# A placement of planned steps on five queues, and a third place on chip for the last sequence's results

## The chip, the cores and the metric

One core of a Trainium2 chip runs the whole program. The metric is the device time of one execution in microseconds (us). The engines are PE (TensorE: matmuls and transposes), DVE (VectorE), ACT (ScalarE), POOL (GpSimd) and SP (SyncE, which here only issues DMAs). Each takes its instructions in the order in which they were written for it, and waits at semaphores.

## The reference, cut to what matters

Eight sequences of 512 tokens go through attention and then through a mixture of experts, each between two layernorms and with a residual.

```python
def attention(x, W_q, W_k, W_v, W_o):                 # x: (8, 512, 256), 16 heads of 16
    Q, K, V = (split_heads(x @ W.T) for W in (W_q, W_k, W_v))
    Q, K = rope(Q), rope(K)
    score = where(causal, -inf, einsum('bnqd,bnkd->bnqk', Q, K) / sqrt(16))
    out = einsum('bnqk,bnkd->bnqd', softmax(score), V)
    return merge_heads(out) @ W_o.T

def ffn(x):                                           # 16 experts of width 128, top 4 in 2 of 4 groups
    scores = sigmoid(x @ gate_w.T)
    topk_idx, topk_w = grouped_top4(scores + gate_bias, scores)      # weights normalized, times 2.5
    y = sum over the 4 experts e of a token: w_e * (silu(x @ Wg[e].T) * (x @ Wu[e].T)) @ Wd[e].T
    return x + y + (silu(x @ Ws_g.T) * (x @ Ws_u.T)) @ Ws_d.T

x = x + layernorm(attention(layernorm(x)))
x = x + layernorm(ffn(layernorm(x)))
```

## The kernel before

The program has three stretches. In the first, attention, the shared expert and the routing run for sequence after sequence (0 to 8, called s), as a pipeline over 32 quads of heads (Q = 4s to 4s+3). In the second, expert blocks of 128 rows go through in duos (BT1, BGU, BT2, BDN): 48 duos for group 0 (sequences 0 to 4), then 32 for group 1 (sequences 5 to 7). The results of group 0 are summed and normalized between the duos of group 1; those of group 1 come last, in a third stretch of their own.

**What sets the order.** `make_plan()` gives each step a time in units of its own (12 a sequence, 3 a quad) and sorts them; every engine then walks the one list PLAN and issues its own part of each step. So a number in the tables BEFORE and AFTER moves a step on all engines that have a part in it, SP too. The steps that matter here, by name:

- LX loads x of a sequence (SP). QK 0 and QK 1 are the two halves of queries and keys: products on PE, four rotary products on DVE (L770 to L774), sums on POOL (L669, L671). SPL splits them into a high part (ACT, `part`, which first waits until the store of the half before has landed) and a low part (POOL, L676). SPS stores them to memory (SP, L522). STL is the stacking load of one quad back from there, eight DMAs (SP, L536 to L539).
- S is a score unit on PE with its row maxima on DVE (L781). MT turns a quad's maxima into rows (PE, ACT, DVE L1081) and SP writes them into `q_st` with four small DMAs (L547). ST is the transposed scores unit with its exponential on ACT (L1189); the first ST of a quad waits for that quad's MT rows. AV and OT make the attention output.
- AT and OP are the output projection (AT: low halves of it on DVE, L799). LNA takes the projection's statistics on DVE, POOL the root. LNB is `residual()`: four rows (L819), one sum (L823), and then the statistics of that sum (L803 to L809). LNC makes the normalized rows, HT transposes them.
- DP is `place_rows()` on DVE, SC are its sixteen scatters on POOL (L691). GE is `group_table()` on DVE, with DUM and PAD the zero rows on SP, WE the load of all expert weights (6144 KB).
- PE's first three PSUM places are a ring for S, ST, XT, QK, V, AT, OP, HT, GU and SD: each waits until the step three places before has been read.

**The last stretch.** `sums(g)` lists it: CZ loads z and x1 of a sequence back (SP, L600 and L601), CL the four experts' rows of half a sequence (SP, L613, 1024 KB), CA adds them (for group 1 on PE, L1380, eight products a half, and then DVE L1016), CS takes statistics, CN makes the final rows (DVE L1046, L1049), and SP stores them (L618). `ykt`, `zt` and `x1t` have two places, by s % 2: sequence 7 takes those of sequence 5, so its CL 7 0 and CL 7 1 wait for CN 5 0 and CN 5 1, and CZ 7 waits until both stores of sequence 5 have landed.

## Time and profile before

| | us |
|---|---|
| median of 3 runs | 1031.69 |
| lowest, highest | 1030.8, 1032.27 |
| time of the profiled execution | 1031.85 |
| its span in the profile | 1030.0 |
| PE busy, share of the span | 830.4, 81% |
| DVE busy, share | 654.9, 64% |

The span runs from the first to the last instruction that the profiler saw; 1.85 us of the execution lie around it. Times in the trace are from the span's start. A row of a timeline begins with the start and the duration of an instruction (or of several alike, "x8"), then come the engine, the line, the operation and the tiles (out<-in); the brackets at its end tell how long the engine had been idle, and who released it.

### The profile page before, as it was taken

What the parts mean: (1) busy time and instruction counts of PE and PEld (TensorE: products, weight loads), DVE (VectorE), ACT (ScalarE), POOL (GpSimd) and SP (SyncE); (2) the same over time, 40 slices, a digit from 0 to 9 for tenths busy, and PEclk for the clock granted to TensorE, in tenths of its full rate; (3) what the DMA queues carried; (4) which work ended last, traced back from release to release, by engine and by line L of the source; (5) the groups of instructions that cost most, each with busy time, mean ns of one, the idle gap of its engine ahead of it and who ended that gap; (6) DMA issues with size and microseconds to landing.
All of it is one profiled execution on the core that took longest, in us unless ns stands there. A gap on an engine that the chain in (4) does not pass through costs nothing.

```text
span 1030.0 us, 20612 instructions
## 1 busy us (share of the span) xinstructions
PE 830.4 (81%) x6580; PEld 610.5 (59%) x6580; DVE 654.9 (64%) x1906; ACT 452.2 (44%) x763; POOL 434.8 (42%) x416
## 2 busy tenths in 40 slices
PE   3449887896898798698796887799988999988763
PEld 3326454564565465466464555688877788777521
DVE  4375758687687787777777694554553333877543
ACT  2115544553544455363464555555444455444300
POOL 4431203115425425424522424467567655655610
PEclk9758989899898899898898898899999999998977
DMA  4475744334444443533559422354556667988663
GB/s 164 118 189 149 226 109 126 81 84 138 127 112 116 130 123 118 136 102 98 157 156 304 138 88 91 109 177 150 175 172 217 201 168 265 337 302 305 237 234 123
DMA packets 89175, 168.72 MB, mean 164 GB/s; under 512 B 14704, under 2 KB 56688, under 8 KB 88816
## 3 DMA queue, kind: packets, MB, share of 16 engines
q1 hardware_dynamic: 75248, 128.85, 43.7%
q0 software_dynamic: 13824, 38.55, 9.9%
q8 instruction: 57, 0.93, 0.4%
q14 instruction: 46, 0.38, 0.1%
HBM read 90.15 MB, written 76.68 MB: 162 GB/s over the span
## 4 chain that ended last, share of the span: by engine, by line
PE 27%; DVE 12%; DMA 6%; issue 5%; SPq 4%; POOL 3%; ACT 2%; DVEq 0%; ACTq 0%; POOLq 0%
PE ring L1480 7%; PE ring L1501 3%; DVE nmax L781 3%; DMA xg<-sorted_rows 2%; PE ring L1259 2%; DMA ykt<-expert_rows 2%; PE ring L1466 2%; PE ring L1261 2%; PE ring L1260 2%; POOL expert_rows L699 2%; PE ring L1380 2%; SPq L592 2%; PE ring L1337 1%; DMA expert_rows<-ys,dest 1%; SPq L593 1%
## 5 line engine op out<-in xcount | busy, mean ns | idle before, releaser
L1189 ACT ACTIVATE prob<-ring 128x1024 f32<-128x1024 f32 (+1 forms) x192 | 167.4, 880 | 208.1 <-PE ring L1328 207.8
L781 DVE TENSOR_REDUCE nmax<-ring 128x2 f32<-128x1024 f32 (+3 forms) x256 | 200.8, 818 | 43.5 <-PE ring L1310 41.6
L699 POOL DMA_INDIRECT expert_rows<-ys,dest x160 | 157.7, 985 | 96.9 <-ACT ys L1143 40.5
L691 POOL DMA_INDIRECT sorted_rows<-xr,idx_all x128 | 131.0, 1023 | 79.7 <-DVE xr L940 46.6
L1480 PE MATMUL ring<-we,xh 128*128 x640 | 155.1, 386 | 0.0
L1480 PEld LDWEIGHTS ring<-we,xh 128*128 128x128 f32 x640 | 118.3, 195 | 13.3
L1003 DVE SCALAR_TENSOR_TENSOR sl<-sl,got,ring 128x128 f32<-128x128 f32 x160 | 48.3, 344 | 104.1 <-ACT sl L1241 103.8
L1322 PE MATMUL ring<-maskt_b,halves_b 64*128 64x128 bf16 (+2 forms) x768 | 57.2, 229 | 63.6 <-DVE nmax L781 37.0
L669 POOL TENSOR_TENSOR rot<-rot 128x512 f32<-128x512 f32 x16 | 20.4, 1278 | 204.6 <-DVE rot L773 204.6
L1322 PEld LDWEIGHTS ring<-maskt_b,halves_b 64*128 64x128 bf16 x768 | 22.5, 96 | 133.2 <-DVE nmax L781 53.7
L1337 PE MATMUL ring<-prob,v_sb 128*32 128x512 f32 (+3 forms) x1024 | 97.9, 481 | 1.7 <-ACT prob L1189 1.7
L1303 PE MATMUL ring<-k_st,q_st 48*128 48x512 f32 (+3 forms) x512 | 84.9, 370 | 17.5 <-ACT prob L1189 9.8
L1328 PE MATMUL ring<-q_st,k_st 50*128 50x384 f32 (+3 forms) x512 | 90.0, 389 | 0.0
L1501 PE MATMUL ring<-we,ah 128*128 x320 | 84.4, 387 | 1.3 <-ACT ys L1143 1.3
L1241 ACT ACTIVATE sl<-ring 128x256 f32<-128x256 f32 x80 | 30.7, 383 | 87.7 <-PE ring L1480 87.7
L1303 PEld LDWEIGHTS ring<-k_st,q_st 48*128 48x128 f32 x512 | 49.3, 210 | 29.0 <-ACT prob L1189 18.1
L1143 ACT ACTIVATE ys<-ring 128x512 f32<-128x512 f32 x80 | 47.8, 598 | 40.6 <-PE ring L1501 34.8
L1466 PE MATMUL ring<-kc,xg 128*128 128x128 f32 x320 | 51.0, 284 | 15.9 <-DMA xg<-sorted_rows 15.9
L1310 PE MATMUL ring<-mask_b,halves_b 64*128 64x128 bf16 (+2 forms) x768 | 60.4, 239 | 0.0
L1143 ACT ACTIVATE xh<-ring 128x512 f32<-128x512 f32 x80 | 47.4, 593 | 28.1 <-PE ring L1466 28.0
L1501 PEld LDWEIGHTS ring<-we,ah 128*128 128x128 f32 x320 | 55.2, 193 | 6.8 <-issue 2.1
L1466 PEld LDWEIGHTS ring<-kc,xg 128*128 128x128 f32 x320 | 40.5, 146 | 26.6 <-DMA xg<-sorted_rows 20.0
(194 smaller groups left out, 1673.7 us busy)
## 6 DMA issues: line engine op xcount, KB each, us to landing
xg<-sorted_rows SPq DMA_DIRECT2D x160, 134.0 KB, 2.5
parts<-part SPq DMA_DIRECT2D x32, 512.0 KB, 5.8
ykt<-expert_rows SPq DMA_DIRECT2D x16, 1024.0 KB, 9.4
k_st<-parts SPq DMA_DIRECT2D x64, 128.0 KB, 3.6
q_st<-parts SPq DMA_DIRECT2D x64, 128.0 KB, 3.5
we<-w_exp SPq DMA_DIRECT2D x1, 6144.0 KB, 21.9
sorted_rows<-zeros SPq DMA_DIRECT2D x2, 2144.0 KB, 12.0
sorted_rows<-zeros SPq DMA_DIRECT2D x32, 134.0 KB
```

Of the source, the lines that this page charges most:

```text
L691: pool.indirect_dma_start(out=xs[group_of(s)], out_offset=bass.IndirectOffsetOnAxis(ap=idx_all[:, s, t, k:k + 1], axis=0), in_=xr[:, s % 2 ...
L699: pool.indirect_dma_start(out=yk, out_offset=bass.IndirectOffsetOnAxis(ap=dest[:, j % 8, b:b + 1], axis=0), in_=ys[:, j % NYS, b, :], in_o ...
L781: dve.tensor_reduce(nmax[:, Q % 2, :, pp, qb], slot[:, :, col:col + (qb + 1) * P], AX.X, ALU.max, negate=True).then_inc(s_max, 1)
L1143: act_e.activation(dst, src, ACT.Copy).then_inc(done, 1)
L1189: act_e.activation(prob[:, u % 2, 2 * half:2 * half + 2, 0:width], slot[:, :, 0:width], ACT.Exp, scale=SCALE).then_inc(s_exp, 1)
L1303: pe.matmul(slot[:, par, col:col + width], q_st[r, Q % NQ, pp, q0:q0 + P], k_st[r, Q % NQ, pp, 0:width], start=n == 0, stop=False, skip_gr ...
L1322: pe.matmul(blocks_of(slot[:, par, :], diagonal)[:, :, 0:64 * (h + 1)], halves_b[r, h, :], mask, start=h == 0, stop=False, skip_group_chec ...
L1328: last = pe.matmul(slot[:, par, col:col + width], k_st[r, Q % NQ, half, k0:k0 + P], q_st[r, Q % NQ, half, k0:T], start=False, stop=True, s ...
L1337: last = pe.matmul(O_BANK[32 * j:32 * j + 32, kb * P:T], v_sb[:, s % 2, kb, 4 * q + j, :], prob[:, u % 2, j, col:col + T - kb * P], start= ...
L1466: last = pe.transpose(X_BANK[:, b, k, :], xg[:, j % NXG, b, k * P:(k + 1) * P], ident)
L1480: last = pe.matmul(G_BANK[j % 2][:, b, :], xh[:, j % 2, b, k, :], we_cols[:, bass.ds(columns[j, b] + k * D, D)], start=(k == 0), stop=(k = ...
L1501: last = pe.matmul(Y_BANK[:, b, :], ah[:, j % 2, b, :], we_cols[:, bass.ds(columns.pop((j, b)) + KD * D, D)], start=True, stop=True)
```

## The change

- `residual()` is cut in two: LNB keeps the rows and the sum, the new step LNS takes the statistics. LNB moves from 25.25 to 24.7, LNS stands where LNB stood. POOL's root for it goes with LNS.
- LX, QK, SPL and SPS of both halves move forward by 0.6 to 0.8 units. DP and SC move back by 0.4 (DP is now behind the low halves of AT), GE by 0.45.
- The last sequence has a third place for `ykt`, `zt` and `x1t`, over the weights and operands of the first stretch. For group 1 `sums()` now lists all CZ, then all six CL, and then the sums.

```diff
-BEFORE = [("LX", -25), ("LN", -20.9), ("LNR", -19.2), ("XT", -16), ("QK", 0, -14.6), ("SPL", 0, -13.6), ("SPS", 0, -12.9),
-          ("QK", 1, -12.8), ("SPL", 1, -11.4), ("SPS", 1, -10.6), ("V", -5)]
-AFTER = [("X1L", 18), ("AT", 22), ("OP", 23), ("LNA", 24), ("LNB", 25.25), ("LNC", 26), ("HT", 27),
+BEFORE = [("LX", -25.6), ("LN", -20.9), ("LNR", -19.2), ("XT", -16), ("QK", 0, -15.2), ("SPL", 0, -14.2), ("SPS", 0, -13.5),
+          ("QK", 1, -13.4), ("SPL", 1, -12.1), ("SPS", 1, -11.4), ("V", -5)]
+AFTER = [("X1L", 18), ("AT", 22), ("OP", 23), ("LNA", 24), ("LNB", 24.7), ("LNS", 25.25), ("LNC", 26), ("HT", 27),
...
-AFTER += [("SD", 30.5), ("Z", 30.501), ("CNT", 32.2), ("DP", 33.9)]
-AFTER += [("SC", n // TOPK, n % TOPK, 34.5 + 0.55 * n) for n in range(NT * TOPK)]
+AFTER += [("SD", 30.5), ("Z", 30.501), ("CNT", 32.2), ("DP", 34.3)]
+AFTER += [("SC", n // TOPK, n % TOPK, 34.9 + 0.53 * n) for n in range(NT * TOPK)]
...
+    if end == B:
+
+        steps = [("CZ", g, s) for s in range(first, end)] + [("CL", g, *half) for half in halves]
+        for i, (s, h) in enumerate(halves):
+            steps += [("CA", g, s, h), ("CS", g, s, h)]
+            if i:
+                steps.append(("CN", g, *halves[i - 1]))
+        return steps + [("CN", g, *halves[-1])]
...
-        add(per_seq * (b - 1) + late(b - 1, 34.3) + FILL, "GE", g)
+        add(per_seq * (b - 1) + late(b - 1, 34.75) + FILL, "GE", g)
...
+        cursor[0] = w_low
+        ykt_last = place("ykt_last", [P, NT, TOPK, D])
+        zt_last = place("zt_last", [P, NT, D])
+        x1t_last = place("x1t_last", [P, NT, D])
+        assert cursor[0] <= w_high
...
-        s_cl = [sem(f"parts_back{i}") for i in range(4)]
-        s_cz = [sem(f"residuals_back{i}") for i in range(2)]
+        s_cl = [sem(f"parts_back{i}") for i in range(6)]
+        s_cz = [sem(f"residuals_back{i}") for i in range(3)]
...
+        def home(s):
+
+            return 2 if s == B - 1 else s % 2
+
+        def turn(s):
+
+            return 1 if s == B - 1 else s // 2 + 1
+
+        def back(s):
+
+            if s == B - 1:
+                return ykt_last, zt_last, x1t_last
+            return ykt[:, s % 2, :, :, :], zt[:, s % 2, :, :], x1t[:, s % 2, :, :]
...
             def load_residuals(s):
-                if s >= 2:
-                    sp.wait_ge(s_out[s % 2], 32 * (s // 2))
+                _, z_home, x1_home = back(s)
+                if turn(s) > 1:
+                    sp.wait_ge(s_out[home(s)], 32 * (turn(s) - 1))
...
-                if s >= 2:
+                if turn(s) > 1:
                     sp.wait_ge(s_cn, N_OUT * (2 * (s - 2) + h + 1))
...
-                elif kind in ("LNA", "LNB"):
-                    post_rstd(n, int(kind == "LNB"))
+                elif kind in ("LNA", "LNS"):
+                    post_rstd(n, int(kind == "LNS"))
...
                 dve.tensor_tensor(x1[:, :, :], x1[:, :, :], pr[:, :, :], ALU.add).then_inc(s_ln, 1)
-                dve.wait_ge(s_ln, done + NT + 1)
-                statistics(x1, s_ln, done + NT + 1, st2, mv2, ve2, s_lnv)
+
+            def residual_statistics(s):
+                done = N_LN * s + 3 * NT + 1
+                dve.wait_ge(s_ln, done)
+                statistics(x1, s_ln, done, st2, mv2, ve2, s_lnv)
...
-                pe.wait_ge(s_cl[2 * (s % 2) + h], 16 * (s // 2 + 1))
+                pe.wait_ge(s_cl[2 * home(s) + h], 16 * turn(s))
```

What is not shown replaces `s % 2` by `home(s)` or `back(s)` in the last stretch's functions.

**SP near the start of the program**, from the load of x of sequence 2 to the first rows of maxima (MT 0). `parts<-part` is SPS, `k_st` and `q_st` from `parts` are STL (quads 2 and 3). Before:

```order
L512 DMA x_ln<-x 128x4x256
L522 DMA parts<-part 64x4x512 x2
L536 DMA k_st<-parts 16x1024
L537 DMA k_st<-parts 32x1024
L538 DMA q_st<-parts 32x1024
L539 DMA q_st<-parts 16x1024
...
L522 DMA parts<-part 64x4x512 x2
...
L547 DMA q_st<-mrow 1x8x128 x4
```

and with the change:

```order
L543 DMA x_ln<-x 128x4x256
L553 DMA parts<-part 64x4x512 x4
L567 DMA k_st<-parts 16x1024
L568 DMA k_st<-parts 32x1024
L569 DMA q_st<-parts 32x1024
L570 DMA q_st<-parts 16x1024
...
L578 DMA q_st<-mrow 1x8x128 x4
```

The store of the second half now stands ahead of the eight loads of quad 2, which stood between the two stores; the same happens in each later sequence, where the rows of maxima of quad 4s-5 stood between the two stores as well.

**DVE at the residual of sequence 4** (`x_67` is x1). Before:

```order
L793 TENSOR_TENSOR att<-ring,rden 128x4x64 [waits attention_transposed,denominators]
L781 TENSOR_REDUCE nmax<-ring 128x2 [waits scores] x2
L1081 TENSOR_TENSOR mrow<-ring,mrow 16x128 [waits maxima_high]
L819 TENSOR_SCALAR pr<-pr,mv_91,rstd_93 128x256 [waits ln_rstd]
L819 TENSOR_SCALAR pr<-pr,mv_91,rstd_93 128x256 x3
L823 TENSOR_TENSOR x_67<-x_67,pr 128x1024 [waits ln_steps,x1_loaded]
L803 BN_STATS st_90<-x_67 128x6 [waits ln_steps]
L803 BN_STATS st_90<-x_67 128x6 x3
L807 BN_AGGR mv_91<-st_90 128x2 [waits ln_steps] x4
L809 TENSOR_SCALAR ve_92<-mv_91 128x4 [waits ln_steps]
L781 TENSOR_REDUCE nmax<-ring 128x2 [waits scores]
```

and with the change:

```order
L825 TENSOR_TENSOR att<-ring,rden 128x4x64 [waits attention_transposed,denominators]
L813 TENSOR_REDUCE nmax<-ring 128x2 [waits scores]
L851 TENSOR_SCALAR pr<-pr,mv_91,rstd_93 128x256 [waits ln_rstd]
L851 TENSOR_SCALAR pr<-pr,mv_91,rstd_93 128x256 x3
L855 TENSOR_TENSOR x_67<-x_67,pr 128x1024 [waits ln_steps,x1_loaded]
L813 TENSOR_REDUCE nmax<-ring 128x2 [waits scores]
L1116 TENSOR_TENSOR mrow<-ring,mrow 16x128 [waits maxima_high]
L835 BN_STATS st_90<-x_67 128x6 [waits ln_steps]
L835 BN_STATS st_90<-x_67 128x6 x3
L839 BN_AGGR mv_91<-st_90 128x2 [waits ln_steps] x4
L841 TENSOR_SCALAR ve_92<-mv_91 128x4 [waits ln_steps]
L813 TENSOR_REDUCE nmax<-ring 128x2 [waits scores]
```

Rows and sum are one row-maximum and MT earlier, and these two stand between them and the statistics.

**SP at the end of the program**, from the residuals of sequence 6 on. Before:

```order
L600 DMA zt<-z_rows 128x1024 [waits x1_stored,z_stored,out_stored0]
L601 DMA x1t<-x_rows 128x1024
L613 DMA ykt<-expert_rows 128x2x1024 [waits block_scattered2,final_rows,block_scattered1,block_scattered0]
L613 DMA ykt<-expert_rows 128x2x1024 [waits final_rows] x3
L618 DMA out<-zt 128x2x256 [waits final_rows]
L613 DMA ykt<-expert_rows 128x2x1024 [waits final_rows]
L618 DMA out<-zt 128x2x256 [waits final_rows]
L600 DMA zt<-z_rows 128x1024 [waits x1_stored,z_stored,out_stored1]
L601 DMA x1t<-x_rows 128x1024
L613 DMA ykt<-expert_rows 128x2x1024 [waits final_rows]
L618 DMA out<-zt 128x2x256 [waits final_rows] x4
```

and with the change:

```order
L632 DMA zt<-z_rows 128x1024 [waits x1_stored,z_stored,out_stored0]
L633 DMA x1t<-x_rows 128x1024
L632 DMA zt_last<-z_rows 128x1024 [waits x1_stored,z_stored]
L633 DMA x1t_last<-x_rows 128x1024
L645 DMA ykt<-expert_rows 128x2x1024 [waits block_scattered2,final_rows,block_scattered1,block_scattered0]
L645 DMA ykt<-expert_rows 128x2x1024 [waits final_rows] x3
L645 DMA ykt_last<-expert_rows 128x2x1024 x2
L650 DMA out<-zt 128x2x256 [waits final_rows] x4
L650 DMA out<-zt_last 128x2x256 [waits final_rows] x2
```

All loads of the last sequence stand ahead of the first store, and none of them waits for a result of sequence 5.

## Rows read from the trace of the kernel before

**Rows 1.** Chain that ended last, 955 to 1031 us: start, duration, what.

```profile
970.43 6.08 DMA expert_rows<-ys,dest
...
978.72 2.38 DMA expert_rows<-ys,dest
...
985.96 12.53 PE ring L1380 x24
...
1001.99 2.91 DMA out<-zt
...
1005.77 7.17 DMA ykt<-expert_rows
...
1012.98 5.80 PE ring L1380 x8
```

**Rows 2.** Timeline of the last stretch.

```profile
968.14 0.93 SPq L601 DMA_DIRECT2D x1t<-x_rows  x1
...
998.59 0.69 DVE L1016 TENSOR_TENSOR ykt<-ring,zt 128x512 f32<-128x512 f32 x1
...
1001.94 0.69 DVE L1016 TENSOR_TENSOR ykt<-ring,zt 128x512 f32<-128x512 f32 x1
```

**Rows 3.** Timeline near the start, SP, ACT and PE.

```profile
57.01 1.84 SPq L536 DMA_DIRECT2D k_st<-parts  x1
...
62.26 1.15 ACT L1143 ACTIVATE part<-rot 128x512 fp32r<-128x512 f32 x2 [8.99 <-DMA parts<-part]
...
65.49 1.24 SPq L522 DMA_DIRECT2D parts<-part  x2
...
66.78 1.96 SPq L536 DMA_DIRECT2D k_st<-parts  x1
...
73.20 0.42 SPq L539 DMA_DIRECT2D q_st<-parts  x1
73.67 2.90 SPq L547 DMA_DIRECT2D q_st<-mrow  x4
...
77.83 0.34 PE L1322 MATMUL ring<-maskt_b,halves_b 64*128 64x64 bf16 x4 [5.94 <-DMA q_st<-mrow]
```

**Rows 4.** Timeline around the second halves of sequence 2.

```profile
110.42 2.50 POOL L676 TENSOR_TENSOR part<-rot,part 128x512 fp32r<-128x512 f32 x2 [2.98 <-ACT part L1143]
...
116.93 1.94 SPq L570 DMA_DIRECT2D sorted_rows<-zeros  x1
...
119.00 4.90 SPq L536 DMA_DIRECT2D k_st<-parts  x1
...
129.15 2.76 SPq L547 DMA_DIRECT2D q_st<-mrow  x4
...
134.65 0.34 PE L1322 MATMUL ring<-maskt_b,halves_b 64*128 64x64 bf16 x4 [4.17 <-DMA q_st<-mrow]
```

**Rows 5.** Timeline of sequence 4's projection and residual, then sequence 5's rows.

```profile
474.73 0.50 PE L1322 MATMUL ring<-maskt_b,halves_b 64*128 64x128 bf16 x4 [2.65 <-DVE h_lo L799]
...
492.37 2.50 POOL L676 TENSOR_TENSOR part<-rot,part 128x512 fp32r<-128x512 f32 x2
492.43 3.69 DVE L819 TENSOR_SCALAR pr<-pr,mv,rstd 128x256 f32<-128x256 f32 x4
...
500.67 0.34 PE L1322 MATMUL ring<-maskt_b,halves_b 64*128 64x64 bf16 x4 [5.06 <-DVE nmax L781]
...
565.64 1.46 DVE L819 TENSOR_SCALAR pr<-pr,mv,rstd 128x256 f32<-128x256 f32 x4
```

**Rows 6.** Timeline of PE, its waits at later places that the change touches.

```profile
552.79 0.58 PE L1259 MATMUL ring<-w_hi,h_lo 128*128 128x256 f32 x1 [5.14 <-DVE nmax L781]
...
561.90 0.26 PE L1322 MATMUL ring<-maskt_b,halves_b 64*128 64x64 bf16 x4 [1.30 <-DMA q_st<-mrow]
...
635.15 1.94 PE L1273 MATMUL ring<-kc,xr 128*128 128x128 f32 x8 [3.82 <-DVE xr L832]
...
753.80 0.44 PE L1493 MATMUL ring<-kc,sl 128*128 128x128 f32 x2 [2.76 <-DVE sl L1003]
```

More of the change, by code:

```diff
@@ L467, in block_kernel @@
         s_cn = sem("final_rows")
-        s_out = [sem(f"out_stored{i}") for i in range(2)]
+        s_out = [sem(f"out_stored{i}") for i in range(3)]
         RELEASE = {
@@ L611, in load_sums @@
                 per_token = yk[first:first + T // 2 * TOPK, :].rearrange("(t p k) d -> p t (k d)", p=P, k=TOPK)
-                dst = ykt[:, s % 2, NHALF * h:NHALF * h + NHALF, :, :].rearrange("p t k d -> p t (k d)")
-                sp.dma_start(dst, per_token).then_inc(s_cl[2 * (s % 2) + h], 16)
+                dst = back(s)[0][:, NHALF * h:NHALF * h + NHALF, :, :].rearrange("p t k d -> p t (k d)")
+                sp.dma_start(dst, per_token).then_inc(s_cl[2 * home(s) + h], 16)
             def store_out(s, h):
@@ L617, in store_out @@
                 tiles = slice(NHALF * h, NHALF * h + NHALF)
-                sp.dma_start(rows(out[s])[:, tiles, :], zt[:, s % 2, tiles, :]).then_inc(s_out[s % 2], 16)
+                sp.dma_start(rows(out[s])[:, tiles, :], back(s)[1][:, tiles, :]).then_inc(s_out[home(s)], 16)
             load_x(0)
@@ L655, in _ @@
                     store_out(st[2], st[3])
-            for par in range(2):
-                sp.wait_ge(s_out[par], 32 * (B // 2))
+            for place_of in range(3):
+                sp.wait_ge(s_out[place_of], 32 * max(turn(s) for s in range(B) if home(s) == place_of))
         @block.gpsimd
@@ L1007, in final_sums @@
                 tiles = slice(NHALF * h, NHALF * h + NHALF)
-                y = ykt[:, s % 2, tiles, :, :]
+                y, z_home = back(s)[0][:, tiles, :, :], back(s)[1]
                 done = sums_before(s, h)
@@ L1011, in final_sums @@
                     if h == 0:
-                        dve.wait_ge(s_cz[s % 2], 32 * (s // 2 + 1))
+                        dve.wait_ge(s_cz[home(s)], 32 * turn(s))
                     n = 2 * (s - SHARED) + h
@@ L1015, in final_sums @@
                     total = ring[2][:, n % 2, :].rearrange("p (t d) -> p t d", t=NHALF)
-                    dve.tensor_tensor(y[:, :, 0, :], total, zt[:, s % 2, tiles, :], ALU.add).then_inc(s_cs, 1)
+                    dve.tensor_tensor(y[:, :, 0, :], total, z_home[:, tiles, :], ALU.add).then_inc(s_cs, 1)
                     return
@@ L1031, in final_statistics @@
                 for t in range(NHALF * h, NHALF * h + NHALF):
-                    dve.bn_stats(st3[:, t, :], ykt[:, s % 2, t, 0, :]).then_inc(s_cst, 1)
+                    dve.bn_stats(st3[:, t, :], back(s)[0][:, t, 0, :]).then_inc(s_cst, 1)
                 for n in range(NHALF):
@@ L1044, in final_rows @@
                 dve.wait_ge(s_cr, 2 * s + h + 1)
+                y_home, z_home, x1_home = back(s)
                 for t in range(NHALF * h, NHALF * h + NHALF):
-                    dve.tensor_scalar(zt[:, s % 2, t, :], ykt[:, s % 2, t, 0, :], mv3[:, t, 0:1], rstd3[:, t:t + 1],
+                    dve.tensor_scalar(z_home[:, t, :], y_home[:, t, 0, :], mv3[:, t, 0:1], rstd3[:, t:t + 1],
                                       ALU.subtract, ALU.mult).then_inc(s_cn, 1)
                 dve.wait_ge(s_cn, done + NHALF)
-                dve.tensor_tensor(zt[:, s % 2, tiles, :], zt[:, s % 2, tiles, :], x1t[:, s % 2, tiles, :],
-                                  ALU.add).then_inc(s_cn, 1)
+                dve.tensor_tensor(z_home[:, tiles, :], z_home[:, tiles, :], x1_home[:, tiles, :], ALU.add).then_inc(s_cn, 1)
             dve.memset(zeros[:, :], 0.0).then_inc(s_init, 1)
@@ L1089, in _ @@
                     residual(n)
+                elif kind == "LNS":
+                    residual_statistics(n)
                 elif kind == "LNC":
@@ L1379, in sum_results @@
                 for k in range(TOPK):
-                    last = pe.matmul(ring[2][:, n % 2, :], ident, ykt[:, s % 2, NHALF * h:NHALF * h + NHALF, k, :],
+                    last = pe.matmul(ring[2][:, n % 2, :], ident, back(s)[0][:, NHALF * h:NHALF * h + NHALF, k, :],
                                      start=k == 0, stop=k == TOPK - 1)
```

6 lines of the change are left out of this document (4 added, 2 removed).

## The prediction

> **What bounds the kernel now.** I read three views in turn: the chain that ended last, for the end of the program, where nothing runs beside it; the timeline of PE with its waits, for the two stretches before; and the timeline of SP, ACT and POOL around each step that the change moves. The profiled execution took 1031.85 us, 1.85 over its span and 0.16 over the median of 1031.69. I add up changes to the span and take them off the median.
>
> In the last stretch the chain [rows 1] shows four halves summed one after another on PE, and then a break: the store of sequence 5's last half has to land (1001.99, 2.91 us), the expert rows of half 7 1 are fetched (1005.77, 7.17 us), and PE starts again at 1012.98. That second start also runs slowly: 5.80 us for eight products, where in steady work a half follows a half every 3.35 us (1001.94 less 998.59 [rows 2]).
>
> At the start PE waits once 5.94 us and once 4.17 us for rows of maxima that SP writes [rows 3, 4]. Before the first, those rows were queued on SP behind eight loads of a quad (66.78 to 73.67); before the second, behind zero rows and a quad throttled by them (116.93 to 129.15). Here SP's order is the bound. In between, PE and DVE take turns: PE waits 2.65 us for the low halves of AT behind DP, and 5.06 us for row maxima behind the residual [rows 5].
>
> **The change, part by part.**
>
> *The last sequence's own place.* PE can go on with 7 0 when 6 1 is done, since its rows were queued right behind the others: 1001.94 plus two paces of 3.35 is 1008.6 for the moment at which DVE gets 7 1, against 1012.98 + 5.80 = 1018.8 [rows 1, 2]. What comes after it (sums, statistics, rows, store) is the same. That is 10.1 less. It rests on six loads of 1024 KB feeding PE: four are queued before as well, and PE got 985.96 to 1001.94 out of them without a break. It has a price. The two residual loads of sequence 7 (1024 KB together) are now issued at about 969, behind those of sequence 6 (968.14, 0.93 us to issue [rows 2]), while the last scatters of expert rows go out. One scatter took 6.08 us to land with such loads in flight, and one 2.38 us after them [rows 1], and the last block waits on that landing. The bounds of the price are 0 and 3.7 us (6.08 less 2.38). I take 2.4, nearer to the upper end, since the loads stay in flight over those same scatters. Sum: -7.7.
>
> On this the Trainium skill (page "DMA: Bandwidth & Descriptors", section "Queues, rings and completion order") says that each DMA engine takes turns between the queues it has work for, packet by packet. By that the scatters of POOL's queue would be slowed, but would not wait for SP's loads to drain; the price could then be near 1, and the sum near 1.4 us better. The row of 6.08 us shows the slowing and can't tell the two apart.
>
> *The second store ahead of a quad's loads, sequence 1.* Low parts of the second half can't be ready earlier: ACT waited 8.99 us, to 62.26, until the first half's store had landed, and the second store left at 65.49 [rows 3]. With the change the loads of quad 2, which went out from 57.01 on, start only behind that store. SP then has sixteen loads between 66.78 and the rows of maxima instead of eight. The first eight cost what eight cost there, 6.9 us (66.78 to 73.67), the other eight at least 3.8 (0.47 each, 73.20 to 73.67) and at most 6.9 again. PE's wait that ends at 77.83 becomes longer by that: +3.8, bounds 0 (the store alone throttles, and lands early) and +6.9. Nothing covers it: PE takes its instructions in order, and the work ahead of this wait is done.
>
> *The same in sequence 2.* The low part ends at 112.92 (110.42 + 2.50 [rows 4]). Store, 1.2 us; loads of quad 6, 3.8 to 6.9; rows of maxima of quad 3, 2.9: the zero rows leave at 121 to 124 and not at 116.93. They throttle the loads of quad 7 (4.90 for the first [rows 4]), and behind those are the rows for which PE waited until 134.65. So +4.0 to +7.1; I take +5.5, the middle, since eight loads straight behind a store cost 6.9 in one place only. ACT gives away a part of this too: its copies of the second half now stand ahead of an exponential, and wait for a store to land.
>
> *Steady sequences, 0 to 4: QK, LNB, DP.* (a) DP behind AT frees the ring place for PE, and the 2.65 us wait [rows 5] goes. But DVE then has DP and the four rotary products of QK 1 ahead of the next row maxima, and the output projection on PE waits for those. QK 1's products are done earlier, though, so PE reaches the next exponentials at about the same time. (b) The residual's rows took 3.69 us beside POOL's low parts and 1.46 us without them [rows 5]; the low parts now come first on POOL, so 2.2 us go. But POOL's root for the projection stands behind those low parts, and starts about 1 to 2 us later, for which the rows wait. (c) One row-maximum and MT stand ahead of the statistics: PE's wait of 5.06 us is cut in two and not shortened, since DVE does the same work until the maxima behind them. I take 0 for the five, bounds -1 and +1 for each.
>
> On (b) the Trainium skill (page "SBUF — State Buffer", section "Who interferes with whom") says that such a vector operation and one of GpSimd exclude each other for a whole instruction, whichever starts first. By that all of the 2.2 us would be won; what the later root takes back, the page doesn't say. The rows of 3.69 and 1.46 us agree with it.
>
> *Sequence 5.* GE no longer stands ahead of a row maximum, and the wait of 5.14 us at 552.79 [rows 6] shrinks to about 1. What is late next is shown by the wait at 561.90: it ends when rows of maxima land behind the load of all expert weights, whose issue does not move. So nearly all is waited for there instead. DVE is ahead by then, and its residual can start sooner: -1.0, bounds -3.8 and 0.
>
> *Sequence 6.* There the residual no longer waits for MT; the wait of 3.82 us at 635.15 [rows 6] loses some 1.5 of it (bounds 0 and -1.9, the time by which its rows can start sooner). *Group 1's table.* DP and GE are parted by a duo, so that the wait of 2.76 us at 753.80 [rows 6] mostly goes: -2.0, bounds 0 and -2.8.
>
> Sum: -7.7 + 3.8 + 5.5 + 0 - 1.0 - 1.5 - 2.0 = -2.9. **Forecast: 1031.7 - 2.9 = 1028.8.** Its own range is 1024 to 1034, from the bounds of the terms, which are not all off to one side.
>
> **Rivals.**
>
> *The opening absorbs its delay* (the landings come early enough, or the waits of 5.94 and 4.17 us were longer than needed). Half or all of the 9.3 us goes: 1019.5 to 1024. For it: the upper bounds of both terms assume that eight loads cost again what eight cost while everything started at once. Against: PE's two waits end on exactly the rows that are pushed back.
>
> *Slower: the same SP order bites in every sequence.* In sequences 3 to 7 store, eight loads and then rows of maxima follow each other too, some 11 us (1.2 + 6.9 + 2.9), where the rows went out at once before, and ACT's copies wait for the first store ahead of an exponential. It decides from the point at which the rows land later than the first transposed scores of that quad are due. Each microsecond over costs one, five times: 1.7 each would give 1037. Against it: once projection and shared expert are in the pipeline, PE and DVE have more work to a quad than at the start, and SP's list has not grown by as much.
>
> *The residual wins all that POOL took.* If the root is not late, 2.2 us in four sequences, 8.9 in all: 1020. This is what the page on SBUF would give.
>
> *The end gives less.* PE drops to the slow pace again (5.80 a half), or the scatters pay the whole 3.7: 3 to 6 us less gain, 1032 to 1035.
>
> *It doesn't do what it says*: the new place is the old weights' place, and could make a load wait. Those are read last in the first stretch, with the whole second stretch between; little speaks for it.
>
> **How the numbers follow.** Forecast 0.46, opening absorbed 0.20, slower in every sequence 0.17, residual wins all 0.08, end gives less 0.06, not as said 0.03. A difference under 0.2% (2.1 us) can't be told from no change. Below 1029.6 lie 0.26 of the forecast's case and nearly all of the second and fourth: 0.55. Within 0.2%: 0.18 of the forecast and 0.05 of others: 0.23. Slower: 0.02 of it, 0.15 of the third, 0.05 of others: 0.22. The range that leaves out no more than 2 in 10 is 1020 to 1037.
>
> **What would show it.** In the new profile: the last six halves on PE without a break, and the span's end some 11 us behind the start of the sum of 7 1; the last scatters landing later than 981; PE's first wait for rows of maxima ending near 82 and its next near 144, which is the step I am least sure of in size; the time between one sequence's residual and the next unchanged, with two waits of PE at the residual instead of one; `pr` rows at 1.4 to 1.6 us throughout; the wait at 552.79 small and that at 561.90 larger. If the opening's waits stay as they are, my main cost is wrong; if the period changes by more than 1 us, my zero is.

## The result, and the profile after

| | us | ratio to the kernel before |
|---|---|---|
| before, median (with its later runs) | 1032.0 | |
| changed, median of 4 (1014.7 to 1024.0) | 1018.2 | 0.987 (0.982 to 0.992) |
| changed, run again (e1), median of 6 (1012.5 to 1021.1) | 1017.9 | 0.986 (0.983 to 0.988) |

The change is worth some 14 us, 1.4%. The forecast was 1028.8 with a range of 1020 to 1037: the direction was right, the gain forecast was about a fifth of what was measured, and the time lies under the range. The first profile of the changed kernel is of its slowest run (1023.98 us, span 1022.2), that of e1 of a quicker one (span 1014.7); both are used.

Where the time went, by marks in the timelines: the first exponential of quads 7 and 24 (ACT; 186.09 and 527.80 before, 196.19 and 530.87 in the changed kernel's first profile, 192.73 and 526.79 in e1), the first expert rows on ACT (676.00 before), the issue of the first load of expert rows at the end (SP, 981.15 before), and the span's end. A minus is time won against the kernel before.

| stretch | forecast | changed, first profile | e1 |
|---|---|---|---|
| start to quad 7 | +9.3 | +10.1 | +6.6 |
| quad 7 to 24, steady | 0 | -7.0 | -7.7 |
| quad 24 to the first expert rows | -2.5 | -3.1 | -4.9 |
| duos | -2.0 | +1.2 | -0.2 |
| last loads to the end | -7.7 | -9.0 | -9.1 |
| sum | -2.9 | -7.8 | -15.3 |

Most of what was not foreseen is in the steady stretch. What answers to [rows 1, 2] follows: DVE's first and last sum before, then the chain and DVE's sums of the changed kernel.

```profile
991.71 0.69 DVE L1016 TENSOR_TENSOR ykt<-ring,zt 128x512 f32<-128x512 f32 x1 [20.67 <-PE ring L1380]
...
1018.81 0.69 DVE L1016 TENSOR_TENSOR ykt<-ring,zt 128x512 f32<-128x512 f32 x1 [5.50 <-PE ring L1380]
```

```profile
971.38 6.26 DMA expert_rows<-ys,dest
...
979.86 2.36 DMA expert_rows<-ys,dest
...
982.28 4.96 DMA ykt<-expert_rows
...
987.28 20.39 PE ring L1417 x40
```

```profile
994.04 0.69 DVE L1051 TENSOR_TENSOR ykt<-ring,zt 128x512 f32<-128x512 f32 x1 [22.04 <-PE ring L1417]
...
1007.78 0.69 DVE L1051 TENSOR_TENSOR ykt_last<-ring,zt_last 128x512 f32<-128x512 f32 x1
1011.13 0.69 DVE L1051 TENSOR_TENSOR ykt_last<-ring,zt_last 128x512 f32<-128x512 f32 x1
```

No store and no second fetch stands in the chain any more. First sum to last took 1018.81 - 991.71 = 27.1 us before, and takes 17.1 now. The two scatters landed in 6.08 and 2.38 us before and in 6.26 and 2.36 now, and from the last expert rows on ACT to the issue of the first load it was 4.56 us before and 4.55 now. What the stretch lacks of 10 us lies behind that: from the first load's issue to the first sum it took 10.56 us before, 11.76 in this profile and 11.59 in e1.

What answers to [rows 3, 4], PE's waits at the opening of the changed kernel:

```profile
76.23 0.80 PE L1340 MATMUL ring<-k_st,q_st 48*128 48x512 f32 x2 [7.31 <-DMA q_st<-parts]
...
81.07 0.34 PE L1359 MATMUL ring<-maskt_b,halves_b 64*128 64x64 bf16 x4 [2.93 <-DMA q_st<-mrow]
...
129.57 0.29 PE L1359 MATMUL ring<-maskt_b,halves_b 64*128 64x64 bf16 x4 [3.49 <-DMA q_st<-mrow]
...
142.65 0.26 PE L1359 MATMUL ring<-maskt_b,halves_b 64*128 64x64 bf16 x4 [2.65 <-DMA q_st<-mrow]
```

The first row is a wait that the forecast did not have: PE now stands 7.31 us in a score unit of quad 2, ahead of the wait for rows of maxima, since that quad's loads went out behind the second store. The wait for rows of maxima behind it ends 3.2 us later than 77.83. The last one ends 8.0 later than 134.65, and the one of 3.49 us, before it, had no wait in its place before. What answers to [rows 5] is in e1, around sequence 4's residual, on PE, POOL and DVE:

```profile
496.22 0.34 PE L1359 MATMUL ring<-maskt_b,halves_b 64*128 64x128 bf16 x4 [2.85 <-DVE nmax L813]
499.44 0.34 PE L1359 MATMUL ring<-maskt_b,halves_b 64*128 64x64 bf16 x4 [2.38 <-DVE nmax L813]
```

```profile
487.52 2.51 POOL L708 TENSOR_TENSOR part<-rot,part 128x512 fp32r<-128x512 f32 x2 [4.81 <-ACT part L1180]
...
491.20 1.04 POOL L713 TENSOR_TENSOR rstd<-ve,minus_half 128x4 f32<-128x4 f32 x1
```

```profile
475.07 0.42 DVE L972 TENSOR_TENSOR weq<-weq,cw 128x256 f32<-128x256 f32 x1
...
489.71 0.35 DVE L841 TENSOR_SCALAR ve<-mv 128x4 f32<-128x4 f32 x1
...
492.28 1.41 DVE L851 TENSOR_SCALAR pr<-pr,mv,rstd 128x256 f32<-128x256 f32 x4 [1.00 <-POOL rstd L713]
```

The low parts end on POOL at 490.03, as the variance (`ve`) gets ready; one scatter stands between, the root starts at 491.20, some 1.1 us late, and the rows wait 1.00 us for it. But they take 1.41 us and not 3.69. A second row that the forecast did not count, a product of DP, takes 0.42 us. Before it took 1.46 in each of the sequences 0 to 3; in sequence 3:

```profile
471.57 1.46 DVE L937 TENSOR_TENSOR weq<-weq,cw 128x256 f32<-128x256 f32 x1
```

What answers to [rows 6] in the first profile:

```profile
551.52 0.39 PE L1296 MATMUL ring<-w_hi,h_lo 128*128 128x256 f32 x1 [2.37 <-DVE nmax L813]
...
564.58 0.34 PE L1359 MATMUL ring<-maskt_b,halves_b 64*128 64x64 bf16 x4 [4.97 <-DMA q_st<-mrow]
...
696.47 1.94 PE L1310 MATMUL ring<-kc,xr 128*128 128x128 f32 x8 [3.88 <-DVE xr L867]
...
758.30 0.44 PE L1530 MATMUL ring<-kc,sl 128*128 128x128 f32 x2 [0.50 <-DVE sl L1038]
```

As forecast, the wait at GE shrank (5.14 to 2.37, where about 1 was said) and the one for rows behind the load of all weights grew (1.30 to 4.97). The wait at group 1's table went (2.76 to 0.50), but a wait for the last sequence's rows took its place (0.98 to 3.88).

### The profile page after: what moved, and what is told of

Its sections match the earlier page's. It is cut to its first block, busy times and chain, and to the rows that moved or that the text cites. A ratio compares the mean times of both kernels' runs of the same rounds, so it can differ in the third digit from the quotient of the medians.

```text
span 1022.2 us, 20612 instructions
## 1 busy us (share of the span) xinstructions
PE 837.2 (82%) x6580; PEld 612.9 (60%) x6580; DVE 640.0 (63%) x1906; ACT 452.9 (44%) x763; POOL 435.9 (43%) x416
## 4 chain that ended last, share of the span: by engine, by line
PE 28%; DVE 9%; DMA 7%; issue 4%; SPq 4%; POOL 3%; ACT 3%; DVEq 0%; ACTq 0%; POOLq 0%
PE ring L1517 8%; PE ring L1538 4%; DMA xg<-sorted_rows 4%; PE ring L1503 2%; PE ring L1296 2%; DVE nmax L813 2%; PE ring L1417 2%; PE ring L1298 2%; PE ring L1297 2%; POOL expert_rows L731 2%; SPq L623 2%; DMA q_st<-mrow 1%; DMA expert_rows<-ys,dest 1%; PE ring L1374 1%; SPq L624 1%
## 5 line engine op out<-in xcount | busy, mean ns | idle before, releaser
L708 POOL TENSOR_TENSOR part<-rot,part 128x512 fp32r<-128x512 f32 x32 | 40.3, 1282 | 45.5 <-ACT part L1180 45.5
## 6 DMA issues: line engine op xcount, KB each, us to landing
ykt<-expert_rows SPq DMA_DIRECT2D x14, 1024.0 KB, 9.9
```

## The steady sequence, side by side

One sequence, from its residual's rows to the next one's, sums it up. A row gives the stretch, its length, then the busy time of PE, PE's weight loads, DVE, ACT and POOL, PE's granted clock, the DMA share and GB/s. Before, the changed kernel, e3 (QK, SPL and SPS at their old numbers), e6 (SPL and SPS alone) and e4 (the residual not split):

```profile
411.60:492.43 80.83, 66.50 (x634) 46.76 (x628) 60.71 (x153) 38.16 (x56) 32.56 (x30) 0.87 0.43 114
```

```profile
418.80:497.30 78.50, 65.12 (x640) 45.01 (x636) 57.44 (x153) 38.14 (x55) 32.51 (x30) 0.91 0.45 117
```

```profile
412.70:494.70 82.00, 66.88 (x636) 46.18 (x636) 62.34 (x153) 38.20 (x56) 31.52 (x29) 0.85 0.44 112
```

```profile
416.80:498.80 82.00, 67.16 (x636) 46.54 (x636) 62.16 (x153) 38.32 (x56) 31.56 (x29) 0.88 0.44 112
```

```profile
407.80:483.00 75.20, 63.41 (x640) 43.33 (x636) 57.44 (x152) 38.18 (x56) 32.69 (x30) 0.93 0.47 122
```

DVE does the same work in all five, and is busy 57.4 us where no operation of it meets POOL's low parts, and 60.7 to 62.3 where one does. PE does the same work too, and is busy 63.4 to 67.2 us, in the order of its clock (0.93 to 0.85), with e6 a little off. So a sequence can lose in three ways at once: DVE beside POOL, PE at the lower clock behind its waits, and PE waiting. The five profiles are not of equal runs: that of e3 is of its slowest run, those of e4 and e6 of their fastest.

## The experiments

**e1, the changed kernel again.** No edit.

> The changed kernel once more, unchanged, for a second profile: its four times so far lay between 1014.7 and 1024.0, and its profile was of the slowest. If the spread sits in one stretch (the expert duos, where that profile lost 3.5 us at a transposition and got them back later, or the loads of the last sequence), the two profiles differ there and agree up to 660 us. Expected median 1018, steady period 78.5 us again, first exponential of quad 7 about 10 us later than before.

1017.9 us. The period is 78.0 to 78.4 again. The spread does not sit in one stretch, and the expectation that the two profiles agree up to 660 us fails: the first one is 2.7 us behind that of e1 at quad 5, 3.5 at quad 7, 4.1 at quad 24, 5.8 at the first expert rows and 7.3 at the loads at the end. The duos (301.8 and 300.4 us from first to last expert rows) differ least.

**e2, the last sequence's place alone.** The edits of e3, e4 and e5 together:

```diff
-("QK", 0, -15.2), ..., ("LNB", 24.7), ..., ("DP", 34.3), ...
+("QK", 0, -14.6), ..., ("LNB", 25.25), ..., ("DP", 33.9), ...
```

> The kernel before with the third place for the last sequence alone; all numbers of the tables as before. My prediction: -10.1 for the two missing breaks, +2.4 (0 to 3.7) for loads beside the last scatters: 1022 to 1025. If the end alone explains the whole result, 1018. The first two stretches should be those of before, with a period of 80.2 us.

1027.3 us, ratio 0.9949 (0.9922 to 0.9976): 5 us, not the 8 to 10. In its profile first sum to last takes 17.1 us, as in the changed kernel, so the break is gone. But its duos took 306.0 us against 300.6 before. One row of that stretch is a wait of PE of 3.52 us, where it was 0.98 us before:

```profile
694.99 1.94 PE L1310 MATMUL ring<-kc,xr 128*128 128x128 f32 x8 [3.52 <-DVE xr L867]
```

Up to the last duos, where the residual loads of sequence 7 now stand, nothing in the order differs from before. Whether that loss is chance (the other profiles with the new place have 297 to 303 us of duos) isn't settled. By this run's 5 us and the 9 us of the table's last stretch, the end explains a third to two thirds of the result, not all.

**e3, QK, SPL and SPS at their old numbers.**

```diff
-BEFORE = [("LX", -25.6), ..., ("QK", 0, -15.2), ("SPL", 0, -14.2), ("SPS", 0, -13.5),
-          ("QK", 1, -13.4), ("SPL", 1, -12.1), ("SPS", 1, -11.4), ("V", -5)]
+BEFORE = [("LX", -25), ..., ("QK", 0, -14.6), ("SPL", 0, -13.6), ("SPS", 0, -12.9),
+          ("QK", 1, -12.8), ("SPL", 1, -11.4), ("SPS", 1, -10.6), ("V", -5)]
```

> The changed kernel with the old numbers of LX, QK, SPL and SPS. Theory A (the shift only costs, at the opening, as I summed): 10 us less than the changed kernel, 1008, and the steady period stays at 78.5. Theory B (the shift brings the steady gain, because the low parts no longer run beside the residual's rows on DVE): the opening's 10 come back, but the rows take 3.7 us again instead of 1.4 and five periods lose about 1.7 each: 1016 to 1018.

1023.1 us, 0.9906 (0.9879 to 0.9932). Theory A, my forecast's (the shift only costs), falls: without it the kernel is 5 us slower, although the opening is back. Theory B (the shift brings the steady gain) holds, and is too small: the residual's rows meet the low parts again.

```profile
494.65 4.34 DVE L851 TENSOR_SCALAR pr<-pr,mv,rstd 128x256 f32<-128x256 f32 x4
```

```profile
479.58 0.58 PE L1296 MATMUL ring<-w_hi,h_lo 128*128 128x256 f32 x1 [3.74 <-DVE nmax L813]
```

The second row (0.71 us in e1) is the output projection that waits behind DP and the rotary products. The period is 82 us, 3.5 longer than in the changed kernel.

**e4, rows and sum back ahead of their statistics.**

```diff
-("LNB", 24.7), ("LNS", 25.25)
+("LNB", 25.25), ("LNS", 25.2501)
```

> The changed kernel with rows and sum back at the place of their statistics. As I predicted (the wait is only cut in two, not shortened): 1018, same as the changed kernel. If the earlier rows and sum bring the steady gain of 1.7 us a sequence: 1026, and PE waits about 5 us once instead of 2.8 and 2.4.

1014.7 us, 0.984 (0.9816 to 0.9865): 3 us less than with the split by the medians, though this interval overlaps that of e1 (0.9828 to 0.9884), so this run alone does not settle it; e8 does. Both expectations miss: I had called the split neutral, and it costs. PE waits once where it waited twice:

```profile
488.98 0.34 PE L1359 MATMUL ring<-maskt_b,halves_b 64*128 64x64 bf16 x4 [4.34 <-DVE nmax L813]
```

One wait of 4.34 us against 2.85 + 2.38, and 1.7 us less of PE's busy time, since the lower clock is seen less: period 75.2 and not 78.4. At the end of the first stretch it is the other way round. e4 is 10.2 us ahead of e1 at quad 24, 7.1 at quad 30 and 3.5 at quad 31. Between the last two it waits 3.82 us for the normalized rows of sequence 6, where e1 waits 1.78:

```profile
624.15 1.92 PE L1310 MATMUL ring<-kc,xr 128*128 128x128 f32 x8 [3.82 <-DVE xr L867]
```

**e5, DP, SC and GE at their old numbers.**

```diff
-("DP", 34.3), ("SC", ..., 34.9 + 0.53 * n), late(b - 1, 34.75)
+("DP", 33.9), ("SC", ..., 34.5 + 0.55 * n), late(b - 1, 34.3)
```

> The changed kernel with DP, SC and GE back at their old numbers. As I predicted (what goes at the low halves comes back at the next exponentials): 1018 plus 2 for the parting of GE and DP: 1020. If the wait of 2.65 us behind DP was a real loss: its row comes back, the period grows by 1.7 to 2.7 us, and the time is 1028 to 1034.

1018.6 us, 0.9867 (0.9845 to 0.9889): no difference. The wait behind DP is back as 1.54 us, the period is 76.8 to 78.5. The zero for this part holds, though not quite for its reason: beside e1 the steady stretch (quad 7 to 24) is 1.8 us shorter with DP at its old place, and at group 1's table the wait of 2.76 us is back where it was 0.50. Its profile has quad 7 4.9 us later than before, where e1 has 6.6 and the first profile 10.1, all with the same SP order, so the opening's price differs between executions.

**e6, SPL and SPS at their old numbers, QK at the new.**

```diff
-("SPL", 0, -14.2), ("SPS", 0, -13.5), ("QK", 1, -13.4), ("SPL", 1, -12.1), ("SPS", 1, -11.4)
+("SPL", 0, -13.6), ("SPS", 0, -12.9), ("QK", 1, -13.4), ("SPL", 1, -11.4), ("SPS", 1, -10.6)
```

> The changed kernel with the old numbers of SPL and SPS alone; QK keeps its new ones. Theory port (the steady gain comes from the residual's rows no longer running beside POOL's low parts, and the clock that PE keeps for it): the rows take 3.7 to 4.3 us again, the period grows from 78.4 to 80 or more, time 1020 to 1025 even with the opening's store back in place. Theory order (the gain comes from the rotary products ahead of the row maxima on DVE, which take 3.7 us of waiting off PE at the output projection): period stays at 78.4, PE's wait there stays at 0.7, time 1012 to 1014.

1031.0 us, 0.9995 (0.997 to 1.002): all of the gain is gone. Theory order (DVE's order brings the gain) falls. Theory port (the rows lose by meeting POOL's low parts) has its rows and its period of 82, though the time lies above its 1020 to 1025. The root runs first on POOL, then the low parts beside DVE's rows:

```profile
415.76 1.04 POOL L713 TENSOR_TENSOR rstd<-ve,minus_half 128x4 f32<-128x4 f32 x1 [6.64 <-DVE ve L841]
...
418.19 2.50 POOL L708 TENSOR_TENSOR part<-rot,part 128x512 fp32r<-128x512 f32 x2
```

```profile
416.83 4.01 DVE L851 TENSOR_SCALAR pr<-pr,mv,rstd 128x256 f32<-128x256 f32 x3
```

Two things stay open. e6 is 8 us slower than e3 with rows and periods alike; 6.3 of them are there at quad 7 in the profiles (189.64 against 183.37), and no run takes that apart. And SPL and SPS also move ACT's copies and SP's stores, which no run here parts from the low parts; for the low parts speak the rows themselves, and DVE's 62.16 us of busy time for the work that takes it 57.44.

**e7, the opening's SP order undone.** In sequences 1 and 2 only, SPL 1 and SPS 1 go back behind the loads they had passed.

```diff
+            if s in (1, 2) and item[:2] in (("SPL", 1), ("SPS", 1)):
+                t += 0.75
```

> The changed kernel, but in sequences 1 and 2 SPL 1 and SPS 1 go back behind the loads that they had passed. By my prediction's terms the opening gets back 9.3 us: 1008.5, by what the profiles show at quad 7 some 6 us: 1012. PE's wait for the rows of MT 0 ends at 78 and not at 82. If the delay only moved a wait that is there anyway: 1018.

1013.0 us, 0.9814 (0.9785 to 0.9843): 5 us faster than the changed kernel by the medians, with an interval that just overlaps that of e1 (0.9828 to 0.9884).

```profile
77.51 0.34 PE L1362 MATMUL ring<-maskt_b,halves_b 64*128 64x64 bf16 x4 [5.37 <-DMA q_st<-mrow]
...
134.55 0.34 PE L1362 MATMUL ring<-maskt_b,halves_b 64*128 64x64 bf16 x4 [5.46 <-DMA q_st<-mrow]
```

Both waits end where they ended before (77.83 and 134.65), and quad 7 is 1.5 us late, not 4.9 to 10.1. The mechanism was right, and worth some 5 us in the time, not 9.3.

**e8, e7 and the split undone in sequences 0 to 4.**

```diff
+            if s < 5 and item[0] == "LNB":
+                t = 25.2499
```

> e7 and in sequences 0 to 4 also rows and sum back directly ahead of the statistics; sequences 5 to 7 keep the split. If the parts add up (opening -6, split undone -11 by quad 23, without the 7 that the undone split costs after quad 30): 1001 to 1005. If undoing the split only shifts work to a later wait: 1008 to 1012.

1005.1 us (1000.7 to 1008.2), 0.9713 (0.9685 to 0.9741). The parts nearly add up: 13 us faster than the changed kernel, 27 faster than before. Against e7, which differs in the split alone, it is 8 us faster with intervals apart: in sequences 0 to 4 the split costs. Periods are 75.2, 75.3, 75.3 and 77.7.

**e9, QK at its old numbers, SPL and SPS at the new** (and e7's opening).

```diff
-("LX", -25.6), ..., ("QK", 0, -15.2), ..., ("QK", 1, -13.4)
+("LX", -25), ..., ("QK", 0, -14.6), ..., ("QK", 1, -12.8)
```

> e7 with the old numbers of QK and LX, and the new ones of SPL and SPS: the fourth corner beside e3 (both old, 1023.1), e6 (QK new, SPL and SPS old, 1031.0) and e7 (both new, 1013.0). Theory port: the low parts end before the statistics, the residual's rows take 1.4 us, and the time is near that of e7, 1013 to 1016. Theory pair (the two moves only pay together, since the low parts can't be early while their products are late): the rows take over 2 us in some sequences and the time is 1018 to 1023.

From here on the kernel before took 1083 to 1104 us in the runs beside these, not 1032, so only ratios count. By the record e1 to e8 ran on two chips, and e9 to e18 on three others. The ratio is 0.9891 (0.9846 to 0.9937), about e3's. The rows don't meet the low parts (below), and yet the time is not that of e7. Its periods of 80 to 85 us hold the standstills that are told of behind e12, so how much of the gain QK's own place brings stays open.

```profile
338.40 1.41 DVE L854 TENSOR_SCALAR pr<-pr,mv,rstd 128x256 f32<-128x256 f32 x4 [1.00 <-POOL rstd L716]
```

**e10, e8 with the last residual loads behind the expert rows; e11, e8 with DP and SC at their old numbers** in sequences 0 to 4.

```diff
-        steps = [("CZ", g, s) for s in range(first, end)] + [("CL", g, *half) for half in halves]
+        steps = [("CZ", g, s) for s in range(first, end - 1)] + [("CL", g, *half) for half in halves] + [("CZ", g, end - 1)]
```

```diff
+            if s < 5 and item[0] in ("DP", "SC"):
+                t -= 0.4
```

> e8 with the two residual loads of sequence 7 behind the six loads of expert rows and not before the last duos. My price for them beside the last scatters was 2.4 us: 1002.7. By the profiles (last rows on ACT to the first sum: 24.8 us against 23.4 before) it is 0.5 to 1.4: 1004. If they then arrive too late for the sum of 7 0, the chain shows them and nothing is gained: 1005.

> e8 with DP and SC of sequences 0 to 4 back at their old numbers (GE keeps its new one). If the wait of 2.65 us behind DP, with the low clock that follows it, is a loss once the rest is in order: the period grows from 75.3 to 77 or more, time 1012. If it is covered, as the equal times of e5 and the changed kernel suggest: 1004 to 1006.

0.9766 (0.9727 to 0.9805) and 0.9609 (0.9566 to 0.9652), beside a kernel before of 1103.5 us. e8 did not run beside them, so neither can be read against it; between the two, e11 is 16.8 us faster.

**e12, e8 again; e14, e11 again; e15, e14 and e10's loads.**

> e8 once more, unchanged, beside the three below on the same chip. The last three kernels ran on a chip on which the kernel before takes 1103 us and not 1032, so that e10 and e11 have no partner. Expected: 0.971 of the kernel before if this chip is like the first, else the reference for the other three.

> e11 again beside its partner e12: DP and SC of sequences 0 to 4 at their old numbers. Theory covered (as e5 against the changed kernel, 1018.6 and 1017.9): within 2 us of e12. Theory helps (on the slow chip e11 was 1.6% ahead of e10, and its periods were 77.2 against 82.1): 3 us or more faster than e12. Theory wait (2.65 us and a low clock each sequence): 5 to 8 us slower.

> e14 and the residual loads of sequence 7 behind the six loads of expert rows. By my price 2.4 us faster than e14, by the profiles 0.5 to 1.4, and from the last expert rows on ACT to the first sum 23.4 us and not 24.8.

Side by side, with a kernel before of 1083.3 us: e12 0.9883 (0.9833 to 0.9932), e14 0.9752 (0.9704 to 0.98), e15 0.9741 (0.9685 to 0.9797). The same file that was 0.971 as e8 is 0.988 here. Its timelines say where that is lost: idle time of DVE and ACT that no instruction ends, marked "remote" or "issue". Rows of e12:

```profile
285.03 1.29 DVE L818 TENSOR_REDUCE nmax<-ring 128x2 f32<-128x768 f32 x2 [3.37 <-remote]
...
507.82 1.29 DVE L818 TENSOR_REDUCE nmax<-ring 128x2 f32<-128x768 f32 x2 [5.71 <-remote]
...
589.55 0.60 ACT L1231 ACTIVATE prob<-ring 128x512 f32<-128x512 f32 x1 [7.72 <-remote]
```

Of such waits of 1.5 us and more, on PE, DVE, ACT and POOL, e12 has 53, 159 us in all, where the kernel before has 3 (11 us) and e1 has 4 (13 us). Up to quad 12 the profiles of e8 and e12 keep step within 2.6 us; at the last expert rows e12 is 64.6 us behind. The standstills are not scattered at random. Of DVE's 27 or 28 in e10, e12 and e16, each on another chip, 18 come at the same instructions in all three: the row maxima at 363.99 and 507.82 in e12 stand still for 3.4 and 5.7 us, and the same two instructions of DVE for 3.5 and 6.0 us in e10 and for 3.4 and 5.9 in e16. In e8 they wait 1.2 and 1.6 us, for PE. What the engines wait for the trace does not show. DP's old place is worth 15 us beside e12, and nothing on the undisturbed runs (e5): e14 has no standstill of DVE at this place in sequences 1 to 4. It pays in that condition only, and the forecast's rows could not tell it.

The loads of the last residuals: the last expert rows on ACT to the issue of the first load take 4.75 us in e14 (1008.46 to 1013.21) and 4.56 in e15 (1004.13 to 1008.69), 0.2 us apart; the kernel before took 4.56 and the changed one 4.55. So the scatters pay nothing of the 2.4 us that I had taken. From there to the first sum e14 and e15 are alike (10.49 and 10.54 us), and e7, with its loads in the changed kernel's order, takes 10.58. So the 1.0 to 1.2 us that the changed kernel and e1 lose there does not come from those loads alone. The 3.2 us between the medians of e14 and e15 are within their intervals.

**e13 and e17, a filled wait.** In sequences 1 to 5 fourteen products that nobody reads stand on PE ahead of the unit that waits at the residual; their sums are thrown away.

```diff
+                if kind == "ST" and n % QUADS == 2 and 6 <= n <= 22 and st[2:] == (0, 2):
+                    pe.wait_ge(*free_of(("MT", n + 1)))
+                    for _ in range(14):
+                        pe.matmul(M_BANK[:, :], wq_hi[:, 0:P], wq_hi[:, 0:T], start=True, stop=True)
```

> e8 with fourteen products that nobody reads on PE, in sequences 1 to 5 in front of the transposed scores unit that waits 4.3 us for row maxima at the residual; they fill some 3.3 us of that wait. If the low clock behind that wait (6.8 us at the lower level each time) comes from the wait, and costs half its length: the clock stays up there, the period goes from 75.3 to 72 and the time down by up to 3.4 x 5 = 17 us. If DVE is the bound behind the wait anyway (it is what PE waits for), or the clock falls for another reason: same as e12, or slower by what the products overrun.

> e13 again, beside e16. On a chip without those standstills: if the clock is worth what the two profiles show for the first undisturbed sequence (74.2 us against 75.3, with 3.4 us of low clock instead of 10.2): 1.1 x 5 = 5 us faster than e16, about 1000. If half of the low clock is lost time: 3.4 x 5 = 17 faster. If the 10 us between e13 and e12 came from the standstills alone: same as e16.

e13 0.9791 (0.9732 to 0.985) beside e12's 0.9883; e17 0.9791 (0.9745 to 0.9836) beside 0.9847 (0.9798 to 0.9896) of e16, which is e8 once more. That is 10 and 8 us faster, twice the same way. The intervals of the ratios overlap in each pair, but all six times of e13 (1052.0 to 1067.7) lie under all six of e12 (1068.7 to 1076.1), and in the second pair one alone of e16's does not lie over all of e17's. Both profiles around the residual of sequence 1, where neither stands still yet; first e8, its wait and then stretches of 4 us (length, PE busy, granted clock):

```profile
254.10 0.34 PE L1364 MATMUL ring<-maskt_b,halves_b 64*128 64x64 bf16 x4 [4.30 <-DVE nmax L818]
```

```profile
248.00:252.00 4.00, 1.81 (x24) 1.00 0.98 236
252.00:256.00 4.00, 1.90 (x20) 0.62 0.87 263
256.00:260.00 4.00, 4.00 (x38) 0.53 0.76 252
```

Then e13, with the fourteen products in the wait:

```profile
250.46 3.49 PE L1433 MATMUL ring<-wq_hi 128*128 128x512 f32 x14
```

```profile
248.00:252.00 4.00, 4.00 (x43) 1.00 1.00 234
252.00:256.00 4.00, 3.08 (x29) 1.00 0.92 240
256.00:260.00 4.00, 2.96 (x42) 1.00 0.82 224
```

In e8 PE's clock falls to 1.2 GHz behind the wait and stays there while its products queue up; in e13 it stays at 2.4. So the wait does cause the low clock. What it is worth shows in the stretch from the residual of sequence 0 to that of sequence 1, which holds one such wait, by its length, PE's busy time and the clock, first in e8 and then in e13:

```profile
173.00:248.20 75.20, 63.57 (x640) 43.46 (x636) 57.28 (x153) 38.19 (x56) 18.88 (x17) 0.93 0.40 107
```

```profile
174.80:248.90 74.10, 64.67 (x654) 45.33 (x650) 57.13 (x152) 38.08 (x56) 18.85 (x17) 0.98 0.38 105
```

Without the filling e13 is busy 64.67 - 3.49 = 61.2 us, 2.4 less than e8. The stretch is 1.1 us shorter, so about half of it shows. The same stretch in e12, beside e13 in the same runs, takes 75.3 us at a clock of 0.90; in the second pair it takes 76.7 us in e16 and 76.2 in e17. Where the rest goes is not shown in full: in e13 PE still waits 0.88 us for DVE's maxima behind the fourteen products.

**e16, e8 a third time; e18, all of it together.**

> e8 a third time, as the partner of the two below. If this chip runs the kernel before at 1032 us, 0.971 of it; if engines again stand still for times that no instruction ends (160 us of such idle time in e12 against 7 in e8), 0.988.

> e17 with DP and SC of sequences 0 to 4 at their old numbers and the residual loads of sequence 7 behind the expert rows. If DP's old place helps only where engines stand still: e17 less 1 (for the loads), plus 0.8 a period (76.1 against 75.3 in the first): 1003. If it helps everywhere, as 15 us between e14 and e12: 990.

e18: 0.9705 (0.9659 to 0.975), 1052.7 us where the kernel before takes 1088.2 and e16 1070.7. It beats e17 by 10 us, as e14 beat e12 by 15. Its time is the lowest of the runs under standstills; by the ratio e11 is lower (0.9609), beside another time of the kernel before. What e17 and e18 take without them was not measured; there e8 is the best that was, at 1005.1.

## Why the prediction was wrong

- **The steady sequences, taken as 0 with bounds of -1 and +1 each: the step that failed.** From quad 7 to quad 24 the two profiles are 7.0 and 7.7 us shorter. Part (b) saw the collision (3.69 against 1.46 us) and let the later root take the gain back. The root is 1.1 us later, as I had it, but the rows give back only 1.0 of 2.3 for that. e3 and e6 show what the forecast had as a rival of 8 in 100: with the low parts behind the root, the rows take 4.0 to 4.3 us, and the period is 82. The 1.04 us at DP (1.46 to 0.42) were left out altogether; DVE's 60.71 - 57.44 = 3.3 us are these two.
- **The rule of the Trainium skill** (page "SBUF — State Buffer", section "Who interferes with whom"), that such operations of DVE and GpSimd exclude each other, pointed the right way. By it all 2.2 us would be won; the trace agrees, since the rows go from 3.69 to 1.41 us, of which the late root takes 1.0 back. I had cited it and weighed it too low.
- **Part (a)** (DP's wait) was right in its sum: e5 finds no difference. **Part (c)**, the split, was called neutral and costs. Undone everywhere (e4) it gives 10.2 us by quad 24 in the profiles, some 3.2 a period, of which 6.7 are lost again by quad 31, and 3 in the medians; undone in sequences 0 to 4 alone (e8 against e7) it gives 8 us.
- **What the sum had no term for at all is PE's clock.** I counted waits. Behind the wait of 4.3 us at the residual PE's products run at the lower clock (a granted clock of 0.50 from 253 to 259 us in e8, at the residual of sequence 1), so it costs more than its length; 0.87 rose to 0.91 with the change, and 0.93 was there to be had. e13 shows it with the order kept, and prices it at 1.1 us in the one sequence compared.
- **The opening, +3.8 and +5.5.** The mechanism was right at both places, with SP's order as the cause (e7). One sentence of it was not: I had the work ahead of the first wait as done, but a score unit of quad 2 stands there and waits 7.31 us for its own loads. The waits end 3.2 and 8.0 us later; the time gives back some 5 us when the order is undone, for which +9.3 was the mis-sized term. About half of it is absorbed, which is the first rival's case.
- **The end, -7.7.** 27.1 us of sums became 17.1: -10.1 was right to 0.1 us. The price of 2.4 at the scatters is at most 0.2 (4.56 and 4.55 us before and after, 4.75 and 4.56 in e14 and e15). The scatters of 6.1 and 2.4 us were there before and after alike, and in e15, with the residual loads of sequence 7 moved away from them, they took 6.01 and 2.37: a row with loads in flight beside it was read as slowed by them. Another 1.0 to 1.2 us is lost between the first load and the first sum, which the forecast did not have and no run explains.
- **Sequence 5** went the way that was said, one wait shrinking and the other growing, though 5.14 became 2.37 and not about 1. **Sequence 6**: 3.82 became 1.78 us. **Group 1's table** won 2.3 us, and a wait for the last rows took 2.9.

The range failed with its bounds: -1 a sequence was all that it allowed the steady part, 5 us in all, and 7 to 8 were measured. Two other terms were off to the same side, the opening (5 us by e7 for 9.3) and the end (9.0 and 9.1 for 7.7). The direction does not depend on the steady part, since the end's gain alone makes the kernel faster (e2).

## What to carry to other kernels

Where two engines are seen to slow each other down in a row that repeats, price the separation in full first, and only take off what a row shows to be late in its place. A step that repeats deserves more care than one at either end: half a microsecond of error in it counts as often as it runs. Of PE's waits, ask also at which clock it works after them; filling a wait with products that nobody reads is a cheap way to find out.

## What was not expected of the hardware

- One and the same kernel ran at 1032 us on two chips and at 1083 to 1104 on three others. In e12, of the latter, there are 159 us of idle time that no instruction ends, in waits of up to 7.7 us, and 18 of DVE's 28 come at the same instructions on all three. Rankings change with it: DP's old place gained 1.3% there (e14 against e12) and nothing on the others (e5 against e1).
- PE's wait of 4.3 us was followed by a granted clock of 0.53 to 0.62 in stretches of 4 us; with 3.5 us of products in it, by 1.00.
- Beside POOL's low parts, DVE's four row operations took 4.35 us at most, against 1.4 alone.
